# Moving 28 transposes from TensorE to transfers, holding back the first output group, and spreading the rounding of a weight, in a two-layer kernel

## The chip, the cores and the metric

The kernel runs on all 8 cores of one Trainium2 chip. Each core computes one of the 8 sequences of the batch, so the cores do the same work on different data and exchange nothing. The metric is the device time of the slowest core in microseconds (us).

## The reference

The reference is a "sandwich": a gated recurrence, then a feed-forward block with ternary weights and 8-bit activations, each behind a layer norm and added to its input.

```
def attn(x, W_in, W_sel_in, W_sel_out, W_out, d):          # per sequence, 4096 x 1024
    u = x @ W_in.T                                          # 256 states
    gates = silu(x @ W_sel_in.T) @ W_sel_out.T              # 4 x 256
    a, b, c, dg = sigmoid, tanh, tanh, sigmoid of the 4 parts
    h_t = a_t * h_{t-1} + (b*u)_t                           # scan over 4096 tokens
    return (c*h + d*dg*u) @ W_out.T

def ffn(x, w1, conv_w, conv_b, w2):
    h = bit_linear(x, w1)                                   # 4096 hidden channels
    h = silu(depthwise_conv1d(h, width 3, padding 1) + b)
    return bit_linear(h, w2)
# bit_linear: activations rounded to 8 bits with the scale of their own token
# (127/max|x|), weights rounded to -1, 0, 1 by their mean magnitude

x = x + layernorm(attn(layernorm(x)))
x = x + layernorm(ffn(layernorm(x)))
```

## The kernel before

All engines run from lists written in one program order; semaphores order them. **Layer one** takes the first 322 us: `half_step(H)` for 128-token groups. In its gaps a generator, `weight_work()`, loads `w1` and `w2` in pieces of 128 x 1024 fp32 (512 KB), sums their magnitudes, and rounds them to fp8 (`rounded`, L533 and L540: a scale-and-add into `kw`, then a Sign on ScalarE). A call of `next(work, None)` takes one step. When layer one ends, 26 pieces of `w2` are still to be rounded.

**Layer two** works in 8 chunks of 512 tokens, each cut into 32 blocks of 128 hidden channels: 256 *slots* n, one a channel block. A slot does, in program order: 8 matmuls of the first product (`w1_mm`, L721), the evacuation to `hp` (ScalarE, L727), the middle tap (ScalarE, L746), the outer taps and sums (VectorE, L753, L760, L765), SiLU for two slots together (L772), running maximum and minimum (VectorE, L780). 38 slots later, since a token's scale needs all its channels, VectorE multiplies and rounds a 128-token piece m = n - 38 (`quant_mul` L833, `quant_rnd` L839, one slot ahead of its use) and TensorE does 8 matmuls of the second product (`w2_mm`, L850). Eight pieces make an output group Gx of 128 tokens, finished by `fin_stats` (VectorE), `fin_chain` (GpSimd), `fin_apply` (ScalarE, then an fp32 addition on GpSimd, L911) and a store. So slots 0 to 37 hold only the first product on TensorE, slots 38 to 255 hold both, and from slot 256 on only the second runs. The convolution shifts the tokens by one: group 0 holds 127 tokens, and the very last token is left over; `last_hidden` and `last_mm` (L953, 64 matmuls whose stationary operand has one column) do it at the end as a group of its own.

**The next chunk's input** is made in between: a group of 128 tokens is centred (GpSimd, L406), reduced (VectorE L411, ScalarE L415), scaled (ScalarE L435), rounded into `xqmB` (VectorE, `quant_x`, L440), transposed by 8 TensorE instructions into PSUM (`quant_T`, L447) and evacuated to `xqT` (ScalarE, `quant_Tev`, L452). In layer two these steps take slots 0 to 6 of every 8 slots (`gq, r = 4 + n // 8, n % 8`), so 4 groups a chunk, 28 in all; chunk 7 has none to make. At a chunk's start 4 small TensorE transposes and 4 small matmuls (L797, L817) make the token scales of the chunk that ended.

The rounding of `w2` takes one step a slot: GpSimd does L533 and ScalarE L540 in slots 0 to 26. Its staging buffers `stgC` and `kw` lie in the memory that the ring `h4` reuses later; the wait at n == 31 guards that. The residual rows `x2r` have two buffers. SyncE (SP) issues all the transfers of layer two in program order, and a wait of one holds back those behind it.

Of the kernel before, what the change touches and what calls it, by code (L numbers as in the profile page):

```python
# [29 lines left out]
class Q:  # L30
# [38 lines left out]
    def dma(self, en, out, in_, sem, *toks):  # L69
        self.wait(en, *toks, (sem, self.cnt.get(sem, 0)))  # L70
        self.cnt[sem] = self.cnt.get(sem, 0) + 16
        self.q[en].append(lambda e, S: e.dma_start(out=out, in_=in_).then_inc(S[sem], 16))  # L72
        return (sem, self.cnt[sem])
# [5 lines left out]
def build_program():  # L79
# [90 lines left out]
    hxq = sb("hxq", 32, BF16)  # L170
    yev = [sb("yev%d" % k, D, F32) for k in range(2)]
    x2r = [sb("x2r%d" % k, D, F32) for k in range(2)]
# [5 lines left out]
    with st_:  # L178
# [8 lines left out]
        hs4 = hs.ap().rearrange("p (f c t) -> p f c t", f=2, c=32)  # L187
        h43 = h4.ap().rearrange("p (c t) -> p c t", c=NH4)
# [266 lines left out]


# [238 lines left out]
        v_q, p_w2 = Z(NW), Z(NW)  # L695
# [160 lines left out]
        def rows(Gx):  # L856

            if Gx == 0:
                return 1, 128, 0
            if Gx == NG:  # L860
                return 0, 1, T_TOK - 1
            return 0, 128, 128 * Gx - 1

        def load_x2(Gx):
            if Gx > NG:
                return
            p0, p1, r0 = rows(Gx)
            x2_ld[Gx] = q.dma("sy", x2r[Gx % 2][p0:p1, 0:D], x2_h[r0:r0 + p1 - p0, :],
                              "x2l%d" % (Gx % 2), g_fo[Gx - 2] if Gx >= 2 else fin_ready[0],
                              v_x2z[0])  # L870

        def fin_stats(Gx):
            np_ = 1 if Gx == NG else 128
            pb = pairW2[Gx % 2]
            for j in range(12):
                sc("bnF", j)
            c0 = col[("bnF", 0)]
            sc("mF", 0), sc("mF", 1)
            c1 = col[("mF", 0)]
            V(lambda e: e.bn_stats(sm[0:np_, c0:c0 + 6], pb[0:np_, 0:512]),  # L880
              v_fs[Gx - 1] if Gx else None, p_w2[8 * Gx + 7] if Gx < NG else p_last[0])
            t = V(lambda e: e.bn_stats(sm[0:np_, c0 + 6:c0 + 12], pb[0:np_, 512:1024]))
            v_fs[Gx] = V(lambda e: e.bn_aggr(sm[0:np_, c1:c1 + 2], sm[0:np_, c0:c0 + 12]), t,  # L883
                         g_fc[Gx - 1] if Gx else None)

        def fin_chain(Gx):
            np_ = 1 if Gx == NG else 128
            f, g, k = Gx // 4, Gx % 4, Gx % 2
            if Gx == NG:
                g2 = sc("g2x")[0:1, :]  # L890
            else:
# [7 lines left out]
            t = G(lambda e: e.tensor_tensor(rs, eF, nhalf[0:np_, :], OP.pow), t)  # L899
            t = G(lambda e: e.tensor_scalar(rF, rs, g2, None, OP.mult), t)  # L900
            g_fc[Gx] = G(lambda e: e.tensor_scalar(bF, mF, rF, none1[0:np_, :], OP.mult, OP.mult), t)  # L901

        def fin_apply(Gx):
            np_ = 1 if Gx == NG else 128
            k = Gx % 2
            pb, Y, X2 = pairW2[Gx % 2], yev[Gx % 2], x2r[Gx % 2]
            a_fa[Gx] = A(lambda e: e.activation(  # L907
                Y[0:np_, :], pb[0:np_, :], AF.Identity, bias=sc("bF", k)[0:np_, :],
                scale=sc("rF", k)[0:np_, :]),
                d_out[Gx - 2] if Gx >= 2 else fin_ready[0], g_fc[Gx])  # L910
            g_fo[Gx] = G(lambda e: e.tensor_tensor(Y[0:np_, :], Y[0:np_, :], X2[0:np_, 0:D], OP.add),  # L911
# [241 lines left out]
```

## Time and profile before

| | us |
|---|---|
| median of 3 runs (lowest, highest) | 1316.98 (1315.31, 1319.25) |
| the profiled execution, its own time | 1316.7 |
| its span, first to last instruction, slowest core (5) | 1315.2 |
| the eight cores' spans | 1308.8 to 1315.2 |
| TensorE, VectorE, ScalarE, GpSimd busy | 89%, 84%, 65%, 32% |

Shares over the whole span hide that the stages differ: layer one is spent on all engines, slots 0 to 37 on VectorE and ScalarE, and slots 38 to 255 on TensorE. The stretches below are cut at the evacuations (L727) that open a slot, so that each holds whole slots.

### The profile page before, as it was taken

The numbers are of one execution on the slowest core, as the hardware profiler recorded it, in microseconds if no ns is written. First come the engines' busy times: TensorE is split into PE (matmuls) and PEld (weight loads), VectorE is DVE, ScalarE is ACT, GpSimd is POOL, SyncE is SP. The second block draws the span as 40 slices with busy tenths as digits, with TensorE's granted clock in tenths as the row PEclk, the third lists the DMA queues.
The fourth block names the chain that finished last, engine by engine and source line by source line (L and its number), as shares of the span: only waits on it lengthen the run. The fifth ranks groups of instructions, "written<-read, shape, count | busy, mean of one in ns | idle before, by whom it ended". The sixth has DMA issues, their size and how long they took to land.

```text
span 1315.2 us, 18619 instructions; the slowest of 8 cores (1308.8 to 1315.2 us)
## 1 busy us (share of the span) xinstructions
PE 1168.4 (89%) x6184; PEld 603.1 (46%) x6184; DVE 1106.9 (84%) x2302; ACT 855.1 (65%) x1131; POOL 419.2 (32%) x654
## 2 busy tenths in 40 slices
PE   0378898997666899999999999999999999999897
PEld 0256666774222444444444444444444444444442
DVE  0269889986999999999999999999999999888661
ACT  0798989998899666666666666666666666555001
POOL 1114222321774122244333224333322431212233
PEclk9998878888898899999999999999999999999898
DMA  9996689995661112111211111121211111010110
GB/s 206 319 331 218 186 256 292 311 310 185 207 198 44 46 39 75 49 48 50 80 49 65 49 49 49 54 76 48 65 49 49 49 51 47 33 33 33 63 67 33
DMA packets 40099, 146.51 MB, mean 111 GB/s; under 512 B 4804, under 2 KB 4804, under 8 KB 39748
## 3 DMA queue, kind: packets, MB, share of 16 engines
q1 hardware_dynamic: 39572, 142.69, 33.8%
q0 software_dynamic: 432, 2.62, 1.2%
q8 instruction: 51, 0.84, 0.2%
q14 instruction: 44, 0.36, 0.1%
HBM read 114.36 MB, written 33.55 MB: 112 GB/s over the span
## 4 chain that ended last, share of the span: by engine, by line
PE 69%; DVE 16%; ACT 5%; DMA 4%; SPq 2%; issue 2%; POOL 1%; POOLq 0%; DVEq 0%; ACTq 0%
PE pF L850 32%; PE pO L721 27%; DMA stg<-w1T 4%; PE pF L326 4%; SPq L72 2%; DVE h L760 2%; PE pO L372 2%; DVE xs L393 1%; DVE h L765 1%; DVE hsc L356 1%; PE pF L953 1%; DVE h L753 1%; PE pT L447 1%; DVE accP L780 1%; DVE ysb L361 1%
## 5 line engine op out<-in xcount | busy, mean ns | idle before, releaser
L850 PE MATMUL pF<-w2q,h 128*128 128x512 fp8e4 x2048 | 480.1, 380 | 1.8 <-DVE h L839 1.8
L721 PE MATMUL pO<-xqT,w1q 128*128 128x512 bf16 x1792 | 427.1, 382 | 5.6 <-ACT xqT L452 5.6
L850 PEld LDWEIGHTS pF<-w2q,h 128*128 128x128 bf16 x2048 | 200.6, 98 | 241.8 <-issue 4.6
L727 ACT ACTIVATE hp<-pO 128x512 bf16<-128x512 f32 x224 | 133.6, 596 | 218.8 <-PE pO L721 217.4
L721 PEld LDWEIGHTS pO<-xqT,w1q 128*128 128x128 fp8e4 x1792 | 175.2, 98 | 213.8 <-issue 10.8
L760 DVE SCALAR_TENSOR_TENSOR h<-hp,cwt,h 128x512 bf16<-128x512 bf16 x256 | 202.8, 792 | 0.7
L746 ACT ACTIVATE bt<-hp,cwt 128x512 bf16<-128x512 bf16 x256 | 183.9, 718 | 6.1
L772 ACT ACTIVATE h<-h 128x1024 bf16<-128x1024 bf16 x128 | 134.9, 1054 | 76.1 <-DVE h L765 75.7
L833 DVE TENSOR_TENSOR h<-h,bc 128x512 bf16<-128x512 bf16 x256 | 151.0, 590 | 0.0
L896 POOL TENSOR_SCALAR sm<-sm 128x1 f32<-128x1 f32 (+1 forms) x33 | 17.2, 522 | 376.6 <-DVE sm L883 376.6
L765 DVE TENSOR_TENSOR h<-h,bt 128x512 bf16<-128x512 bf16 x256 | 115.6, 452 | 14.7 <-ACT bt L746 1.3
L753 DVE TENSOR_SCALAR h<-hp,cwt,cbt 128x512 bf16<-128x512 bf16 x256 | 111.9, 437 | 15.2 <-ACT hp L727 14.7
L911 POOL TENSOR_TENSOR yev<-yev,x2r 128x1024 f32<-128x1024 f32 (+1 forms) x33 | 78.1, 2368 | 45.4 <-ACT yev L907 45.4
L721 PE MATMUL pF<-xqT,w1q 128*128 128x512 bf16 x256 | 66.6, 412 | 29.2 <-ACT hp L727 25.4
L780 DVE TENSOR_TENSOR accN<-accN,h 128x1024 bf16<-128x1024 bf16 x120 | 92.0, 767 | 0.0
L907 ACT ACTIVATE yev<-pF,sm 128x1024 f32<-128x1024 f32 (+1 forms) x33 | 39.6, 1200 | 78.6 <-POOL sm L901 78.6
L780 DVE TENSOR_TENSOR accP<-accP,h 128x1024 bf16<-128x1024 bf16 x120 | 82.1, 684 | 0.1
L741 POOL COPY hs<-hp 128x8 bf16<-128x8 bf16 x64 | 25.8, 403 | 167.4 <-ACT hp L727 167.4
L326 PE MATMUL pF<-selh,wsoT_b 128*128 128x256 bf16 x512 | 70.7, 306 | 4.4 <-ACT selh L319 4.4
L839 DVE TENSOR_SCALAR h<-h 128x512 bf16<-128x512 bf16 x256 | 73.4, 287 | 1.2
L285 PE MATMUL pT<-identb,xn 128*128 128x128 bf16 x256 | 24.6, 253 | 54.1 <-ACT xn L278 52.8
L308 PE MATMUL pF<-xinT,wselT_b 128*128 128x256 bf16 x512 | 65.9, 294 | 0.0
(147 smaller groups left out, 1514.7 us busy)
## 6 DMA issues: line engine op xcount, KB each, us to landing
stg<-w1T SPq DMA_DIRECT2D x40, 512.0 KB, 15.3
xs<-x SPq DMA_DIRECT2D x32, 512.0 KB, 11.2
stg<-w2T SPq DMA_DIRECT2D x32, 512.0 KB, 9.1
x2c<-xs SPq DMA_DIRECT2D x32, 512.0 KB, 9.0
stgC<-w2T SPq DMA_DIRECT2D x32, 512.0 KB, 5.9
x2r<-x2c SPq DMA_DIRECT2D x31, 512.0 KB, 4.6
out<-yev SPq DMA_DIRECT2D x31, 512.0 KB, 3.0
x2q<-x2c SPq DMA_DIRECT2D x28, 512.0 KB, 3.3
```

The lines of the kernel that those rows point to most:

```text
L326: t = P(lambda e, gi_=gi_, m=m, k=k: e.matmul(pF[:, at + 256 * gi_:at + 256 * (gi_ + 1)], wsoT[:, 1024 * k + 128 * m:1024 * k + 128 * (m + ...
L721: p_w1[n] = P(lambda e, k=k: e.matmul(bankW1(n), w1q[:, HD * k + 128 * c:HD * k + 128 * (c + 1)], xT[:, :, k, :], start=(k == 0), stop=(k ...
L727: a_ev[n] = A(lambda e: e.activation(hp3[:, n % 8, 2:514], bankW1(n), AF.Identity), *((v_stt[n - 8], a_bt[n - 8], g_sv[n // 4 - 2]) if n > ...
L746: a_bt[n] = A(lambda e: e.activation(bt[n % 3][:, :], hp3[:, n % 8, 1:513], AF.Identity, scale=cwt[:, 3 * c + 1:3 * c + 2]), v_cv[n - 3] i ...
L753: v_ts[n] = V(lambda e: e.tensor_scalar(H_, hp3[:, n % 8, 0:512], cwt[:, 3 * c:3 * c + 1], cbt[:, c:c + 1], OP.mult, OP.add), p_w2[32 * (o ...
L760: v_stt[n] = V(lambda e: e.scalar_tensor_tensor(H_, hp3[:, n % 8, 2:514], cwt[:, 3 * c + 2:3 * c + 3], H_, OP.mult, OP.add), v_ts[n])
L765: v_cv[n] = V(lambda e: e.tensor_tensor(H_, H_, bt[n % 3][:, :], OP.add), v_stt[n], a_bt[n])
L772: a_si[n] = a_si[n - 1] = A(lambda e: e.activation(pair(n), pair(n), AF.Silu), v_cv[n])
L780: t = V(lambda e: e.tensor_tensor(acc[:, :], acc[:, :], pair(n), o), mm_tok[which], a_si[n])
L833: q_tok[m] = V(lambda e: e.tensor_tensor(piece(m), piece(m), bc2[f % 2][:, 128 * g:128 * (g + 1)].unsqueeze(1).to_broadcast([128, 4, 128]) ...
L850: p_w2[m] = P(lambda e, c=c, jj=jj: e.matmul(pb[:, 512 * jj:512 * (jj + 1)], h43[:, ring(32 * f + c), 128 * g:128 * (g + 1)], w2q[:, D * c ...
L911: g_fo[Gx] = G(lambda e: e.tensor_tensor(Y[0:np_, :], Y[0:np_, :], X2[0:np_, 0:D], OP.add), x2_ld[Gx], a_fa[Gx])
```

## The change

- **Transposes by transfer.** In layer two `quant_T` and `quant_Tev` (8 TensorE instructions, one ScalarE instruction) become `turn_x`: one transposing transfer on SP from `xqmB` to `xqT`. The next `quant_x` and the next chunk's first product wait for its semaphore. The first 4 groups, in layer one, stay on TensorE.
- **Cadence.** The steps of a group now start every 7 slots within the first 28 slots of a chunk (`gq, r = 4 + 4 * f1 + s1 // 7, s1 % 7`).
- **First group held back.** Group 0's rounded values go to a buffer of their own, `held` (m < 8), and its 64 matmuls are not done in slots 38 to 45 but at the very end; the last token takes the place of its unused first column. So `last_mm` and one of 33 finishing groups are gone.
- **Rounding of w2.** The same steps are spread over 42 slots, and the waits move to n == 47. Its buffers and four of `xs` change places in memory.
- **The end.** The last group's application and addition are cut in halves, the addition is on VectorE, and six smaller stores follow (`fin_end`). `x2r` has one buffer and its clearing at n == 31 is gone. In layer one, mean and variance go to small columns instead of behind `xs`.

```diff
@@ transposes
-            if r == 5:
-                quant_T(gq, xqmB, pT1b, pT1_free)
-            if r == 6:
-                quant_Tev(gq, xqT[gq // 4 % 2][:, D * (gq % 4):D * (gq % 4 + 1)], pT1b, pT1_free,
+            if r == 5:
+                turn_x(gq, xqT[gq // 4 % 2][:, D * (gq % 4):D * (gq % 4 + 1)], xqmB,
+        def turn_x(gi, dst, xqm, *toks):
+            p_t2[gi] = a_t2[gi] = q.dma("sy", dst.rearrange("p (k t) -> p k t", k=8), xqm[:, :],
+                                        "tx", v_xq[gi], *toks, turn=True)
-            gq, r = 4 + n // 8, n % 8
-            if gq < NG:
+            gq, r = 4 + 4 * f1 + s1 // 7, s1 % 7
+            if gq < NG and s1 < 28:
@@ the first group
+            dst = held3[:, 4 * m:4 * m + 4, :] if m < 8 else piece(m)
-            if 0 <= m < NW:
+            if 8 <= m < NW + 8:
                 w2_mm(m)
-            if m == NW:
-                last_mm()
@@ w2's rounding
+        left = len(steps) + 1 - at_step[0]
-            next(work, None)
+            if n < 42 and (n + 1) * left // 42 > n * left // 42:
+                next(work, None)
+            if n == 47:
+                q.wait("v", v_w2q[31], *kw_free)
-                v_x2z[0] = V(lambda e: e.memset(x2r[0][0:1, :], 0.0))
@@ the end
-        fin_apply(NG)
-        fin_store(NG)
+        fin_end()
+            for n in range(2):
+                h = slice(512 * n, 512 * (n + 1))
+                t = V(lambda e, h=h: e.tensor_tensor(Y[:, h], Y[:, h], X2[:, h], OP.add),
+                      *x2_ld[Gx], toks[n])
+                for i, (p0, p1, r0) in enumerate(rows(Gx)):
+                    q.dma("sy", out_h[r0:r0 + p1 - p0, h], Y[p0:p1, h], "oe%d" % (3 * n + i), t)
```

TensorE in chunk 1, slots 51 to 54, before: `pO` is the first product, `pF` the second, `pT` the transposes.

```order
L850 MATMUL pF<-w2q,h_111 128x512 x8
L721 MATMUL pO<-xqT_112,w1q 128x512 x8
L850 MATMUL pF<-w2q,h_111 128x512 x8
L447 MATMUL pT<-identb,xqmB 128x128 x8
L721 MATMUL pO<-xqT_112,w1q 128x512 x8
L850 MATMUL pF<-w2q,h_111 128x512 x8
```

And now, the same engine and stage:

```order
L734 MATMUL pO<-xqT_112,w1q 128x512 x8
L868 MATMUL pF<-w2q,h_111 128x512 x8
L734 MATMUL pO<-xqT_112,w1q 128x512 x8
L868 MATMUL pF<-w2q,h_111 128x512 x8
L734 MATMUL pO<-xqT_112,w1q 128x512 x8
```

The eight transposes are gone from between the products.

GpSimd in slots 4 to 12 of chunk 0, before: `kw` is the first half of w2's rounding, `x2q` the centring of a group, `hp` and `hs` the carried columns.

```order
L735 COPY hp<-hs 128x4x2
L533 TENSOR_SCALAR kw_63<-stgC_66,wcons,consts 128x1024
L533 TENSOR_SCALAR kw_64<-stgC_65,wcons,consts 128x1024
L533 TENSOR_SCALAR kw_63<-stgC_68,wcons,consts 128x1024
L533 TENSOR_SCALAR kw_64<-stgC_67,wcons,consts 128x1024
L741 COPY hs<-hp 128x8
L735 COPY hp<-hs 128x4x2
L406 TENSOR_SCALAR x2q_124<-x2q_124,nmean,ones 128x1024
```

And now:

```order
L748 COPY hp<-hs 128x4x2
L543 TENSOR_SCALAR kw_67<-stgC_72,wcons,consts 128x1024
L543 TENSOR_SCALAR kw_68<-stgC_71,wcons,consts 128x1024
L411 TENSOR_SCALAR x2q_124<-x2q_124,nmean,ones 128x1024
L543 TENSOR_SCALAR kw_67<-stgC_70,wcons,consts 128x1024
L754 COPY hs<-hp 128x8
L748 COPY hp<-hs 128x4x2
```

Between two restores (4 slots) stand 2 or 3 roundings instead of 4; the 26 roundings reach into slot 41.

SP around two groups of chunk 2, now (before, only the load of `x2q`, the store and the load of `x2r` stood there):

```order
L73 DMA x2q_124<-x2c 128x1024 [waits dv,xq1]
L73 DMA_TRANSPOSE xqT_112<-xqmB 128x8x128 [waits tx]
L73 DMA out<-yev_129 128x1024 [waits gp,ot0]
L73 DMA x2r<-x2c 128x1024 [waits x2l0]
L73 DMA x2q_123<-x2c 128x1024 [waits dv,xq0]
L73 DMA_TRANSPOSE xqT_112<-xqmB 128x8x128 [waits tx]
```

The transposing transfer stands in the one queue of SP, between loads and stores.

## Rows read from the trace of the kernel before

**Rows 1.** The page: the chain that ended last, shares by engine.
```profile
PE 69%; DVE 16%; ACT 5%; DMA 4%; SPq 2%; issue 2%; POOL 1%; POOLq 0%; DVEq 0%; ACTq 0%
```

**Rows 2.** Windows: stretch, its length, busy of each engine (instructions), clock, DMA.
```profile
351.10:376.05 24.95, 17.23 (x74) 6.49 (x72) 24.36 (x39) 24.15 (x34) 20.10 (x16) 0.93 0.61 190
376.05:400.95 24.90, 17.22 (x74) 6.64 (x72) 24.31 (x39) 24.15 (x33) 20.04 (x16) 0.93 0.55 169
400.95:423.00 22.05, 12.26 (x52) 4.62 (x50) 20.55 (x39) 19.44 (x29) 7.74 (x10) 0.88 0.07 25
423.00:442.87 19.87, 15.36 (x69) 7.50 (x68) 16.17 (x38) 11.41 (x17) 4.64 (x5) 0.79 0.22 73
442.87:470.94 28.07, 28.07 (x137) 12.95 (x138) 27.21 (x64) 18.48 (x27) 4.03 (x7) 1.00 0.07 25
```

**Rows 3.** Windows, the same columns: chunk 2, eight slots with, eight without transposes.
```profile
564.38:678.80 114.42, 113.81 (x557) 52.90 (x556) 107.20 (x237) 72.94 (x101) 38.00 (x53) 1.00 0.17 56
592.45:620.53 28.08, 28.08 (x137) 12.99 (x136) 25.77 (x56) 18.29 (x26) 10.22 (x14) 1.00 0.17 58
1135.00:1162.63 27.63, 27.63 (x129) 12.54 (x128) 24.92 (x55) 15.43 (x22) 6.97 (x12) 1.00 0.12 39
```

**Rows 4.** Timeline, TensorE: start, length; the first transposes behind slot 46 and the last.
```profile
496.83 0.61 PE L447 MATMUL pT<-identb,xqmB 128*128 128x128 bf16 x8
...
1096.98 0.61 PE L447 MATMUL pT<-identb,xqmB 128*128 128x128 bf16 x8
```

**Rows 5.** Timeline, GpSimd and VectorE in slots 14 to 16, and slot 31.
```profile
369.59 4.30 POOL L533 TENSOR_SCALAR kw<-stgC,wcons,consts 128x1024 f32<-128x1024 f32 x2 [1.88 <-ACT w2q L540]
...
370.02 0.75 DVE L760 SCALAR_TENSOR_TENSOR h<-hp,cwt,h 128x512 bf16<-128x512 bf16 x1
371.62 1.22 DVE L753 TENSOR_SCALAR h<-hp,cwt,cbt 128x512 bf16<-128x512 bf16 x1
372.87 1.56 DVE L760 SCALAR_TENSOR_TENSOR h<-hp,cwt,h 128x512 bf16<-128x512 bf16 x1
374.88 0.41 DVE L753 TENSOR_SCALAR h<-hp,cwt,cbt 128x512 bf16<-128x512 bf16 x1
...
421.57 0.91 DVE L1058 MEMSET x2r<- 1x1024 f32 x1 [0.19 <-issue]
```

**Rows 6.** The waits: engine, tile, line, releaser: us, times, longest; second product.
```profile
PE pF L850 <- DVE h L839: 1.8, 2, 1.3
```

**Rows 7.** DMA issues: count, KB each, median us to landing.
```profile
x2q<-x2c SPq DMA_DIRECT2D x28, 512.0 KB, 3.3
x2r<-x2c SPq DMA_DIRECT2D x31, 512.0 KB, 4.6
stgQ<-w1T SPq DMA_DIRECT2D x7, 512.0 KB, 21.2
```

**Rows 8.** Timeline, the last microseconds, and a half-width fp32 operation of VectorE.
```profile
300.92 0.69 DVE L359 TENSOR_TENSOR ch<-bcg,hsc 128x512 f32<-128x512 bf16 x1
...
1291.99 13.97 PE L953 MATMUL pF<-w2q,hxq 128*1 128x512 fp8e4 x64
...
1309.81 1.20 ACT L907 ACTIVATE yev<-pF,sm 1x1024 f32<-1x1024 f32 x1 [12.63 <-POOL sm L901]
1311.09 2.33 POOL L911 TENSOR_TENSOR yev<-yev,x2r 1x1024 f32<-1x1024 f32 x1 [1.31 <-ACT yev L907]
```

**Rows 9.** Timeline, TensorE: a first product at either clock, after a wait and in steady state.
```profile
433.35 3.62 PE L721 MATMUL pO<-xqT,w1q 128*128 128x512 bf16 x8
...
609.52 1.89 PE L850 MATMUL pF<-w2q,h 128*128 128x512 fp8e4 x8
```

More of the change, by code:

```diff
@@ L67, in op, with dma @@
         return (sem, self.cnt[sem]) if inc else None
-    def dma(self, en, out, in_, sem, *toks):
+    def dma(self, en, out, in_, sem, *toks, turn=False):
         self.wait(en, *toks, (sem, self.cnt.get(sem, 0)))
         self.cnt[sem] = self.cnt.get(sem, 0) + 16
-        self.q[en].append(lambda e, S: e.dma_start(out=out, in_=in_).then_inc(S[sem], 16))
+        kind = {"transpose": True} if turn else {}
+        self.q[en].append(lambda e, S: e.dma_start(out=out, in_=in_, **kind).then_inc(S[sem], 16))
         return (sem, self.cnt[sem])
@@ L131, in build_program @@
     place[0] = both_end + 32 * 1024
+    xs = [sb("xs%d" % k, D, F32) for k in range(4)]
     kw = [sb("kw%d" % k, D, F32) for k in range(2)]
@@ L169, in build_program @@
     hx = sb("hx", 64, F32)
-    hxq = sb("hxq", 32, BF16)
+    held = sb("held", 32 * 128, BF16)
     yev = [sb("yev%d" % k, D, F32) for k in range(2)]
-    x2r = [sb("x2r%d" % k, D, F32) for k in range(2)]
+    x2r = sb("x2r", D, F32)
     b_end = place[0]
@@ L262, in ln1_stats @@
             X, k = slot(gi), gi % 2
-            both = cols("bn1", k, 12)
+            both, mv = cols("bn1", k, 12), cols("m1", k, 2)
             old = v_st1[gi - 2] if gi >= 2 else None
@@ L845, in w2_mm @@
             pb = pairW2[Gx % 2]
-            q.wait("t", v_q[m], *(v_w2q[4 * j:4 * j + 4] if m < 8 else ()),
-                   a_fa[Gx - 2] if Gx >= 2 and j == 0 else None)
+            q.wait("t", v_q[m] if Gx < NG else v_hxq[0],
+                   *(v_w2q[4 * j:4 * j + 4] if Gx == 1 else ()),
+                   a_fa[Gx - 2] if Gx >= 3 and j == 0 else None)
             for c in range(4 * j, 4 * j + 4):
+                hid = (held3[:, c, :] if Gx == NG else
+                       h43[:, ring(32 * f + c), 128 * g:128 * (g + 1)])
                 for jj in range(2):
-                    p_w2[m] = P(lambda e, c=c, jj=jj: e.matmul(
-                        pb[:, 512 * jj:512 * (jj + 1)],
-                        h43[:, ring(32 * f + c), 128 * g:128 * (g + 1)],
+                    p_w2[m] = P(lambda e, c=c, jj=jj, hid=hid: e.matmul(
+                        pb[:, 512 * jj:512 * (jj + 1)], hid,
                         w2q[:, D * c + 512 * jj:D * c + 512 * (jj + 1)],
@@ L903, in fin_apply @@
         def fin_apply(Gx):
-            np_ = 1 if Gx == NG else 128
             k = Gx % 2
-            pb, Y, X2 = pairW2[Gx % 2], yev[Gx % 2], x2r[Gx % 2]
+            pb, Y, X2 = pairW2[Gx % 2], yev[Gx % 2], x2r
             a_fa[Gx] = A(lambda e: e.activation(
[L908 to L911, printed above, removed]
-                         x2_ld[Gx], a_fa[Gx])
@@ L945, in last_hidden @@
             t2 = V(lambda e: e.tensor_scalar(X0, X0, mc, RC, OP.mult, OP.add), t2)
[L946 to L958 removed]
+            v_hxq[0] = V(lambda e: e.tensor_scalar(held3[:, :, 0], X0, -RC, None, OP.add), t2, v_q[7])
+        fin_ready = [None]
         load_x2q(4)
```

116 lines of the change are left out of this document (56 added, 60 removed).

## The prediction

> **What bounds the kernel now.** I read the chain of waits first, then the busy time by stretch, then single rows. The chain [rows 1] says TensorE for 69% of the span, but that is an average; the stretches say where. In chunk 0 (slots 8 to 23) VectorE and ScalarE are both busy for 24.1 to 24.4 of 24.9 us per 8 slots, and TensorE for 17.2 [rows 2]. So there eight slots cost what VectorE and ScalarE need, 3.1 us a slot. From slot 38 on the picture turns round: TensorE is busy for all of the 28.07 us of 8 slots, and VectorE for 27.21 in slots 38 to 45 [rows 2] and 107.20 of 114.42 us in a later chunk [rows 3]. The second product waits for VectorE for 1.8 us in the whole span [rows 6]. TensorE is the bound in slots 38 to 255, with VectorE at 94% close behind. The tail (only second products) is TensorE's too.
>
> I make the sum against the profiled execution (1316.7 us, span 1315.2), which is 0.3 us from the median of the runs, 1316.98; a saving in it is taken off the median.
>
> **Transposes.** Eight slots of a chunk with a group to make take 28.08 us, eight slots of the last chunk, which has none, 27.63 [rows 3]: 0.45 us for 8 transposes, though each set shows 0.61 of its own [rows 4], since matmuls overlap their neighbours' ends. From slot 46 to the end of chunk 6 there are 22 such sets, the first and last of them in [rows 4]. TensorE bounds there, so 22 x 0.45 = 9.9 us go, if nothing else is late. What is late next is VectorE: a chunk would take 114.42 - 4 x 0.45 = 112.6 us of TensorE, against 107.2 of VectorE, 95%. The steps of four groups now stand in 28 slots instead of 32, and in slot 22 a reduction falls into the slot in which an output group's statistics are taken. For such bunches I put +1 us over six chunks, with 0 and +5 as the ends. ScalarE loses its evacuations; it has a third of its time free in chunk 2 (72.94 of 114.42), so this gives nothing.
>
> **The transfer that replaces them** is in no row. It moves 256 KB. The nearest rows by size and load are loads of 512 KB that land in 3.3 and 4.6 us at a DMA share of 0.17; the slowest of SP's transfers, under a full load in layer one, take 21.2 us [rows 7]. So I bound it by 1.6 and 21 us and take 5. Its cover: `xqmB` is rewritten 7 slots later, 7 x 3.45 = 24 us, and the last group of a chunk is issued in slot 26 and first read in slot 32, about 20 us. In chunk 0, at 2.9 us a slot, the same distance is 17 us, and TensorE runs a few slots ahead there, which takes it to about 10. At 5 us all of it is hidden; at 21 us only the chunk ends show, 7 x 1 us or so, plus some 10 us once in chunk 0. On SP it waits for `quant_x`, for which the load before it already waits; what stands behind it are the store and the load of `x2r`. The single buffer of `x2r` is loaded in 4.6 us, and its next use is 8 slots (27 us), in the tail 13.8 us, after the last: hidden.
>
> The rows price eight transposes at 0.45 us of TensorE, and the transfer at less than its cover. The Trainium skill speaks against the swap: "VectorE: DVE Perf Modes", section "The three transpose paths", gives 390 ns for a 128 x 128 transpose on TensorE and 1309 ns by transfer, and its rules advise TensorE where PSUM will do. By that eight would be, as an estimate, 10.5 us of transfer; that is still under the cover of 20 to 24 us in the steady chunks, and the sum would stay. No row here shows the transfer.
>
> **The first group.** 64 matmuls leave slots 38 to 45, 13.8 us of TensorE, and 64 return at the end in place of the 64 of the last token (13.97 us [rows 8]). The tail is so unchanged in TensorE. In slots 38 to 45 TensorE would need half of the 28.07 us, but VectorE keeps its 27.21 [rows 2], because the rounding of group 0 is still done there. So of 13.8 us only the 0.86 us by which VectorE was idle can be won: this edit has nearly no worth of its own, and I count it with the next.
>
> **The head, slots 0 to 45.** A rounding of `w2` costs VectorE time too, though it runs on GpSimd and ScalarE: beside an L533 on GpSimd, L753 goes from 0.41 to 1.22 us and L760 from 0.75 to 1.56 [rows 5]. From 350.3 to 375.2 eight operations of VectorE are longer by 5.9 us together, beside 8 roundings and a centring: 0.65 us each. Spreading 26 roundings over 42 slots does not remove this, it moves it: 9 or 10 of them go to slots 27 to 41, 6.3 us of VectorE later for 6.3 us earlier. What can be won is time in which VectorE was idle: 0.59, 0.59, 1.50, 3.70 and 0.86 us in the five stretches of [rows 2], 7.2 us, and the clearing of `x2r` (0.9 us [rows 5]). In the first two stretches ScalarE was as full as VectorE; it now gets 1.05 us x 0.36 less a slot and drops out as a bound. Of the 3.70 us about half are waits across the chunk's end that stay. I take 4.0 us as gained. The ends are -8 us (all of it) and +5 us: if slots 0 to 26 do not get shorter by what leaves them, because something else holds them, the 6.3 us added behind slot 26 remain, less the clearing.
>
> **The clock.** TensorE is half busy until slot 45 instead of slot 37. In 423 to 443 us, busy 15.4 of 19.9, it was granted 0.79, and one set of 8 matmuls took 3.62 us instead of 1.89 [rows 2, 9]; these are the 1.2 and the 2.4 GHz level. If slot 46 opens at the lower one, a set or two cost 1.7 us each: 0 to +3.5, I take +0.5.
>
> **The end.** After the last matmul the chain is as before up to L907 at 1309.81. Then 1.20 + 2.33 us of application and addition [rows 8] become two halves of about 0.6 and two additions of 0.69 (L359), about 2.1 us to the last, against 3.6; three issues more at about 0.35 us and larger stores take back most of the difference. -0.3 (-1 to +0.5).
>
> **Sum.** -9.9 + 1.0 - 4.0 + 0.5 - 0.3 = -12.7 us. 1316.98 - 12.7 = 1304.3.
>
> **The rivals.**
> *VectorE takes over in the steady chunks.* It is at 94%; if bunching or GpSimd work at a new phase adds 5.5 us to its 107.2, the chunk ends at VectorE's time and the transposes give nothing: -12.7 + 8.9 = -3.8, 1313.2. For it: every longer GpSimd operation stretches a VectorE one by 0.8 us [rows 5]. Against: nothing in the change adds VectorE work, and the second product waits for it for 1.8 us in all [rows 6].
> *The head gets longer.* Roundings in slots 27 to 41 are on VectorE's path, and slots 0 to 26 are held by another thing, such as the chain GpSimd, ScalarE, GpSimd of the rounding (waits of 1.88 us before an L533 [rows 5]). Then +5 instead of -4: -3.7, 1313.3. Against: that chain has fewer links per slot now.
> *It gets slower: the transfer outlasts its cover.* Each group waits for the one before through `xqmB`. Over 24 us, every us costs 24 groups 1 us each: at 30 us +139 us in the steady chunks, so some 1450. It turns the gain into a loss from about 24.6 us on. Against: no row of 512 KB took that long, even at a DMA share near 1; for it: no row shows a transposing transfer, and moving elements of 2 bytes could be far slower than rows of 4 KB.
> *The held group pays.* Without second products VectorE and TensorE might pass slots 38 to 45 faster than 27 us, if VectorE's operations there were stretched by waiting rather than by work: up to 7 us more, 1297.3. Against: 27.21 of 28.07 us are busy.
>
> **How the numbers follow.** Forecast 0.66, VectorE takes over 0.12, head longer 0.10, transfer outlasts 0.07, held group pays 0.05. The gaining ends of all terms together are -9.9 - 8 - 1 = -18.9 us, 1298.1, and one more of the losing ends (VectorE's +5 or the head's +5) beside the taken values gives 1313.3 at most; I leave out the transfer's case and two losing ends at once: 1298 to 1313.5. A difference of 0.3% (4 us) is about what a measurement of this kernel tells from none. Faster by more than that: the forecast, the last rival, half of the first two: 0.82; within: 0.11; slower: 0.07.
>
> **What would show it.** In the profile after: eight slots of chunks 1 to 6 at 27.63 us, TensorE busy without gaps, no transposes between them; VectorE at 95 to 97% of a chunk. Slots 8 to 23 at 2.8 to 2.9 us instead of 3.1, with ScalarE at 80 to 90%. Slots 38 to 45 at about 27 us with TensorE half busy. The second product's first matmul about 4 us before 470.9. The transposing transfers landing in under 10 us, and no wait of `quant_x` or the first product for them. Wrong would be: waits of the second product for VectorE of more than 5 us in all, or any wait for `xqT`.

## The result: 0.4% slower, and where it went

The changed kernel takes 1322.56 us (median of 6 runs, 1321.61 to 1323.05) against 1317.14 us of the kernel before beside it: the ratio is 1.0042, 95% interval 1.0031 to 1.0053. Forecast were 1304.3 us and a range that ended at 1313.5. Repeated later on another chip the ratio was 1.0047 (1.0034 to 1.0060). Executions in which the cores of one die ran at a lower granted clock and took some per cent longer are left out of every ratio.

The page of the changed kernel, its first line and the chain that ended last (by engine, then by line):

```profile
span 1321.3 us, 18079 instructions; the slowest of 8 cores (1312.9 to 1321.3 us)
...
DVE 38%; PE 34%; ACT 8%; DMA 7%; issue 6%; POOL 3%; SPq 2%; DVEq 0%; POOLq 0%; ACTq 0%
PE pF L868 17%; PE pO L734 12%; DVE h L773 7%; DVE h L778 5%; DVE h L766 4%; DMA stg<-w1T 4%; DVE accP L793 3%; ACT h L785 3%; DMA x2c<-xs 2%; SPq L73 2%; DVE h L846 2%; DVE xqmB L445 2%; DVE sm L416 2%; PE pF L331 2%; ACT hp L740 2%
```

This is the first thing to see. Before, TensorE had 69% of the chain and VectorE 16% [rows 1]; now VectorE leads with 38%. The chain is no sum of causes, but followed back through 560 to 680 us, which lies in chunks 2 and 3, it says the same of the steady chunks: the two products had 91% of it there and have 23% now. VectorE has taken a large part of TensorE's place.

The windows of the same kernel, cut at the evacuations that open a slot (stretch, length, busy time of TensorE, its weight loads, VectorE, ScalarE, GpSimd with instructions, clock, DMA share, GB/s): slots 8 to 15, 16 to 23, 24 to 31 of chunk 0, then chunk 2 from slot 8 on over 32 slots, and two stretches of 8 slots in it.

```profile
352.51:377.38 24.87, 18.28 (x70) 6.66 (x67) 24.28 (x40) 21.49 (x32) 13.11 (x15) 0.90 0.43 137
377.38:400.44 23.06, 14.45 (x63) 5.75 (x64) 22.09 (x41) 20.37 (x29) 16.05 (x13) 1.00 0.42 127
400.44:422.19 21.75, 13.01 (x51) 4.87 (x48) 21.19 (x34) 19.56 (x27) 13.58 (x10) 0.92 0.55 167
561.75:677.93 116.18, 112.84 (x525) 50.70 (x524) 107.96 (x236) 69.74 (x96) 36.14 (x53) 1.00 0.24 64
590.63:618.44 27.81, 27.81 (x129) 12.39 (x128) 26.79 (x58) 17.06 (x24) 8.88 (x13) 1.00 0.23 67
618.44:648.13 29.69, 27.95 (x129) 12.40 (x128) 27.92 (x63) 16.60 (x23) 9.62 (x16) 1.00 0.22 63
```

Against [rows 3]: 32 slots took 114.42 us and take 116.18, though TensorE's work in them is less. Slots 16 to 23 still run at 27.81, near the 27.63 of the forecast; the next eight need 29.69, with VectorE busy for 27.92 of them and TensorE standing for 1.7.

Cut at slots 48, 224 and 248, the two profiled executions compare like this:

| stretch | before, us | changed, us | difference | forecast |
|---|---|---|---|---|
| layer one, start to slot 0 | 322.34 | 323.37 | +1.0 | 0 |
| head, slots 0 to 47 | 155.70 | 153.25 | -2.5 | -3.5 |
| slots 48 to 223 | 628.22 | 635.72 | +7.5 | -8.9 |
| slots 224 to 247 | 83.99 | 84.00 | 0.0 | 0 |
| slot 248 to the end of the span | 124.91 | 124.97 | +0.1 | -0.3 |

These two executions differ by 6.1 us where 12.7 less was forecast, a miss of 18.8 us, and 16.4 of it stands in slots 48 to 223. The first row is hardly an effect of the change: on one other chip four kernels, two with each version of layer one, reached slot 0 between 317.6 and 319.9 us, at 318.2 in the mean with the new version and at 319.3 with the old.

Inside a chunk the loss has a place. Four slots take 13.8 us when TensorE alone sets the pace (the table's values are differences between starts of evacuations, L727 or L740, in chunk 2; every chunk from 2 to 6 shows the same within 0.4 us):

| slots of the chunk | 0-3 | 4-7 | 8-11 | 12-15 | 16-19 | 20-23 | 24-27 | 28-31 | chunk |
|---|---|---|---|---|---|---|---|---|---|
| before | 14.8 | 15.4 | 13.8 | 14.3 | 13.8 | 14.3 | 13.8 | 14.3 | 114.41 |
| changed | 14.8 | 15.0 | 15.1 | 13.8 | 14.0 | 13.8 | 15.9 | 13.8 | 116.14 |

The transposes' 0.45 us are gone from every eight slots, and two bulges have come, 1.3 us in slots 8 to 11 and 2.1 us in slots 24 to 27. The timeline of the changed kernel in slots 22 to 26 of chunk 2 (start, length, engine, line, what, and the wait before it):

```profile
619.72 0.22 DVE L433 TENSOR_SCALAR sm<-sm 128x1 f32<-128x1 f32 x1 [1.70 <-POOL sm L428]
...
621.76 0.75 DVE L773 SCALAR_TENSOR_TENSOR h<-hp,cwt,h 128x512 bf16<-128x512 bf16 x1
...
622.84 2.81 POOL L912 TENSOR_TENSOR yev<-yev,x2r 128x1024 f32<-128x1024 f32 x1 [2.88 <-ACT yev L909]
...
623.36 2.84 DVE L445 TENSOR_SCALAR xqmB<-x2q,sm 128x1024 bf16<-128x1024 f32 x1
...
627.21 1.89 PE L868 MATMUL pF<-w2q,h 128*128 128x512 fp8e4 x8 [1.60 <-DVE h L853]
```

VectorE waits 1.70 us for the scale of an input group (L428), since GpSimd was doing the chain of an output group (from 616.1 to 618.8); then the long fp32 addition on GpSimd (L912) overlaps the rounding of the input group (L445), which takes 2.84 us instead of 0.75; the piece for the second product is 1.6 us late. In the whole span:

```profile
PE pF L868 <- DVE h L853: 15.9, 12, 1.9
PE pO L734 <- ACT hp L740: 13.2, 6, 4.9
```

The first line was 1.8 us, 2 times before [rows 6]. The visible waits of TensorE understate the loss.

### The profile page after: what moved, and what is told of

It is laid out like the page before. It is cut to its first block, busy times and chain, and to the rows that moved or that the text cites. A ratio compares the mean times of both kernels' runs of the same rounds, so it can differ in the third digit from the quotient of the medians.

```text
span 1321.3 us, 18079 instructions; the slowest of 8 cores (1312.9 to 1321.3 us)
## 1 busy us (share of the span) xinstructions
PE 1136.8 (86%) x5896; PEld 576.1 (44%) x5896; DVE 1109.1 (84%) x2301; ACT 831.0 (63%) x1103; POOL 405.8 (31%) x647
## 4 chain that ended last, share of the span: by engine, by line
DVE 38%; PE 34%; ACT 8%; DMA 7%; issue 6%; POOL 3%; SPq 2%; DVEq 0%; POOLq 0%; ACTq 0%
PE pF L868 17%; PE pO L734 12%; DVE h L773 7%; DVE h L778 5%; DVE h L766 4%; DMA stg<-w1T 4%; DVE accP L793 3%; ACT h L785 3%; DMA x2c<-xs 2%; SPq L73 2%; DVE h L846 2%; DVE xqmB L445 2%; DVE sm L416 2%; PE pF L331 2%; ACT hp L740 2%
## 5 line engine op out<-in xcount | busy, mean ns | idle before, releaser
L868 PE MATMUL pF<-w2q,h 128*128 128x512 fp8e4 x1984 | 464.6, 380 | 16.5 <-DVE h L853 15.9
L868 PEld LDWEIGHTS pF<-w2q,h 128*128 128x128 bf16 x1984 | 191.9, 98 | 255.0 <-issue 32.4
L740 ACT ACTIVATE hp<-pO 128x512 bf16<-128x512 f32 x224 | 132.5, 591 | 142.2 <-PE pO L734 141.2
L773 DVE SCALAR_TENSOR_TENSOR h<-hp,cwt,h 128x512 bf16<-128x512 bf16 x256 | 213.8, 835 | 0.7
L766 DVE TENSOR_SCALAR h<-hp,cwt,cbt 128x512 bf16<-128x512 bf16 x256 | 118.7, 464 | 9.2 <-ACT hp L740 9.2
L846 DVE TENSOR_TENSOR h<-h,bc 128x512 bf16<-128x512 bf16 x256 | 122.6, 479 | 0.0
L899 POOL TENSOR_SCALAR sm<-sm 128x1 f32<-128x1 f32 x32 | 15.7, 490 | 334.1 <-DVE sm L891 334.1
L912 POOL TENSOR_TENSOR yev<-yev,x2r 128x1024 f32<-128x1024 f32 x31 | 79.1, 2553 | 50.0 <-ACT yev L909 49.8
L793 DVE TENSOR_TENSOR accN<-accN,h 128x1024 bf16<-128x1024 bf16 x120 | 90.7, 756 | 0.0
L793 DVE TENSOR_TENSOR accP<-accP,h 128x1024 bf16<-128x1024 bf16 x120 | 83.8, 699 | 0.1
L909 ACT ACTIVATE yev<-pF,sm 128x1024 f32<-128x1024 f32 x31 | 37.2, 1199 | 65.3 <-POOL sm L904 65.3
L377 PE MATMUL pO<-woutT_b,ysb 128*128 128x512 bf16 x128 | 35.3, 400 | 44.4 <-DVE xs L398 43.6
L853 DVE TENSOR_SCALAR h<-h 128x512 bf16<-128x512 bf16 x248 | 71.4, 288 | 1.2
L290 PE MATMUL pT<-identb,xn 128*128 128x128 bf16 x256 | 23.8, 247 | 51.8 <-ACT xn L283 51.0
```

The costliest lines, as they stand in the source:

```text
L740: a_ev[n] = A(lambda e: e.activation(hp3[:, n % 8, 2:514], bankW1(n), AF.Identity), *((v_stt[n - 8], a_bt[n - 8], g_sv[n // 4 - 2]) if n > ...
L766: v_ts[n] = V(lambda e: e.tensor_scalar(H_, hp3[:, n % 8, 0:512], cwt[:, 3 * c:3 * c + 1], cbt[:, c:c + 1], OP.mult, OP.add), p_w2[32 * (o ...
L773: v_stt[n] = V(lambda e: e.scalar_tensor_tensor(H_, hp3[:, n % 8, 2:514], cwt[:, 3 * c + 2:3 * c + 3], H_, OP.mult, OP.add), v_ts[n])
L793: t = V(lambda e: e.tensor_tensor(acc[:, :], acc[:, :], pair(n), o), mm_tok[which], a_si[n])
L846: q_tok[m] = V(lambda e: e.tensor_tensor(piece(m), piece(m), bc2[f % 2][:, 128 * g:128 * (g + 1)].unsqueeze(1).to_broadcast([128, 4, 128]) ...
L868: p_w2[m] = P(lambda e, c=c, jj=jj, hid=hid: e.matmul(pb[:, 512 * jj:512 * (jj + 1)], hid, w2q[:, D * c + 512 * jj:D * c + 512 * (jj + 1)] ...
```

## The experiments

All ratios are against runs of the kernel before on the same chip. Three theories stood against each other: (A) the new cadence of 7 slots lets a group's steps meet an output group's steps; (B) the transposing transfers disturb the other engines; (C) VectorE has no room below 114 us a chunk whatever the order.

**Cadence 8 in the changed kernel** (`e1_cadence8`).

```diff
-            gq, r = 4 + 4 * f1 + s1 // 7, s1 % 7
-            if gq < NG and s1 < 28:
+            gq, r = 4 + n // 8, n % 8
+            if gq < NG:
```

> The changed kernel with the cadence of before (a group's steps in slots 0 to 6 of every 8), everything else as changed. In the changed kernel four slots of a chunk take 13.8 us where nothing stands in the way, but slots 8 to 11 take 15.1 and slots 24 to 27 take 15.9; before no four slots behind slot 8 took over 14.3. Theory A, the cadence: steps of a group meet the statistics and the long addition of an output group in the same slots, and VectorE falls behind. Then both bulges go, a chunk takes 112.7 us instead of 116.1, and the time is 1322.5 - 3.5 x 5.5 = about 1303. Theory B, the transposing transfers disturb VectorE or ScalarE: the chunk stays near 116 and the time near 1322. Theory C, VectorE has no room below 114 us a chunk whatever the cadence: 114.4 us a chunk, about 1312.

Measured: ratio 0.990 (0.988 to 0.992), the profile's span 1298.7 us. Slots 48 to 223 took 618.40 us, 17.3 less than in the changed kernel. The windows of this kernel, chunk 2:

```profile
526.56:639.19 112.63, 112.02 (x525) 51.06 (x524) 104.14 (x236) 69.80 (x96) 38.70 (x53) 1.00 0.22 66
```

The chunk takes 112.63 us, which is the 112.6 of the forecast, and TensorE is busy for all but 0.6 of it. Both bulges are gone with the transfers still there. B and C fall. For a kernel of 1317 us the ratio is 1304, where about 1303 was expected.

**Cadence 7 in the kernel before** (`e2_before_cadence7`), the same two lines the other way round, transposes on TensorE.

> The kernel before with the cadence of 7 slots only; transposes stay on TensorE. Theory A: the same bulges at slots 8 to 11 and 24 to 27, a little smaller as TensorE is slower by 0.45 us a group: a chunk takes 117 to 118 us instead of 114.4, the time is about 1332. Theory B: no bulge, the time stays at 1317. Theory C: VectorE's work is the same, 1317.

Measured: 1.0082 (1.0065 to 1.0099). A chunk took 116.5 us, with 15.6 in slots 24 to 27 and 14.6 in slots 8 to 11. The cadence alone, without any transfer, makes both bulges. They are smaller than expected (1332 was expected, 1.0082 is 1328 for a kernel of 1317); that TensorE's own 0.45 us a group leaves VectorE more room would explain it, but is not shown.

**The transfers alone in the kernel before** (`e3_before_turn`): `turn_x` at r == 5 in place of `quant_T` and `quant_Tev`.

```diff
-                    quant_T(gq, xqmB, pT1b, pT1_free)
-                if r == 6:
-                    quant_Tev(gq, xqT[gq // 4 % 2][:, D * (gq % 4):D * (gq % 4 + 1)], pT1b, pT1_free,
+                    turn_x(gq, xqT[gq // 4 % 2][:, D * (gq % 4):D * (gq % 4 + 1)], xqmB,
```

> The kernel before with the transposing transfers only, cadence 8. Theory A: 0.45 us of TensorE a group go, a chunk takes 112.7 us, the time is 1317 - 10 = 1307. Theory B: bulges where the transfers run, 1322 or more. Theory C: 1317.

Measured: 0.9930 (0.9914 to 0.9947), about 9 us. Slots 48 to 223 went from 628.22 to 618.45 us, 9.8, against 9.9 forecast for the transposes; all 22 sets that the forecast counted lie in these slots. What a transfer costs, by the DMA issues of the changed kernel (count, median us to landing) and the transfers' own lines in the changed kernel with cadence 8 (its issues on SP in ns, its landings min, median, max):

```profile
xqT<-xqmB SPq DMA_TRANSPOSE x28, 4.3
```

```profile
L73 SPq DMA_TRANSPOSE xqT<-xqmB x28: 1237/1237/1751, 336.5 to 1075.1; - x28
...
DMA to landing us min/median/max: 3.1/4.3/6.4
```

**The second and the last start moved, one at a time.** First the last group of a chunk starts in slot 24, the others stay at 0, 7 and 14 (`e5_last_at24`):

```diff
-            gq, r = 4 + 4 * f1 + s1 // 7, s1 % 7
-            if gq < NG and s1 < 28:
+            gq, r = NG, 0
+            for i_, at_ in enumerate((0,7,14,24)):
+                if at_ <= s1 < at_ + 7:
+                    gq, r = 4 + 4 * f1 + i_, s1 - at_
+            if gq < NG:
```

> The changed kernel with its groups starting in slots 0, 7, 14 and 24 of a chunk instead of 0, 7, 14 and 21. If each bulge belongs to one group's start (21 makes slots 24 to 27, 7 makes slots 8 to 11): the bulge at 24 to 27 goes from 15.9 to 13.8 us, the one at 8 to 11 stays at 15.1; a chunk takes 114.0 us and the time is 2.1 x 5.5 = 12 us below the changed kernel, 0.995 of the kernel before. If instead it is the sum of VectorE's work in the chunk, both change.

Measured: 0.9970 (0.9957 to 0.9982), beside the changed kernel's 1.0047 on that chip. In chunk 2, slots 24 to 27 took 13.8 us, slots 8 to 11 stayed at 15.1, the chunk took 114.05. The trace is as forecast. The time fell by 9.8 us (1321.74 to 1311.96, medians), and slots 48 to 223 by 10.2, where I had said 12: 2.1 us in the five chunks 2 to 6 are 10.5, and chunk 1 had no bulge of that size (13.8 us in its slots 24 to 27 in the repeated run of the changed kernel).

Then the second group starts in slot 8, the others stay at 0, 14 and 21 (`e10_second_at8`):

```diff
+            for i_, lo_, hi_ in ((0, 0, 7), (1, 8, 14), (2, 14, 21), (3, 21, 28)):
+                if lo_ <= s1 < hi_:
+                    gq, r = 4 + 4 * f1 + i_, s1 - lo_
```

> The changed kernel with the second group of a chunk starting in slot 8 instead of 7; the others stay at 0, 14 and 21. By the bulge of each start: slots 8 to 11 fall from 15.1 to 13.8 us, slots 24 to 27 stay at 15.9; a chunk takes 114.8 us and the time is 7 us under the changed kernel, 0.999 of the kernel before.

Measured: 0.9982 (0.9972 to 0.9992). Slots 8 to 11: 13.8 us, slots 24 to 27: 15.5, the chunk 114.37, where 114.8 was expected. The bulges are apart and each belongs to one start, but for 0.4 us of the later one, which went with the move of the second group too.

**What in the cadence does it.** The long addition of the output groups on GpSimd is cut to 8 of its 1024 columns (groups 1 to 31; the output lacks the rest), once with cadence 7 (`e7_no_addition`), once with cadence 8 (`e11_cadence8_no_addition`):

```diff
-            g_fo[Gx] = G(lambda e: e.tensor_tensor(Y[:, :], Y[:, :], X2[:, 0:D], OP.add),
+            g_fo[Gx] = G(lambda e: e.tensor_tensor(Y[:, 0:8], Y[:, 0:8], X2[:, 0:8], OP.add),
```

> The changed kernel (cadence 7) without the long fp32 addition of the residual rows on GpSimd in the output groups 1 to 31: it covers 8 of 1024 columns, so the output lacks the rest. In slot 24 that addition (2.8 us) overlaps the rounding of an input group on VectorE, which takes 2.84 us instead of 0.75. If this overlap makes the bulges: the one at slots 24 to 27 falls from 15.9 to 14.3 us or less and the one at 8 to 11 from 15.1 to under 14; a chunk takes 113 us, the time is 1305. If VectorE's own work in a bunch makes them (statistics and reduction in one slot, 2.5 us), the bulges stay above 15 us and the time above 1316.

> The control to the run without the addition: cadence 8 throughout, and the addition of the residual rows covers 8 of 1024 columns in the output groups 1 to 31, so the output lacks the rest. With cadence 7 and without the addition a chunk took 111.76 us. If the cadence costs only through the addition, this is the same: a chunk 111.7 to 111.8 us, 0.987 of the kernel before. If the cadence costs something by itself, it is shorter than that.

Measured: 0.9872 (0.9852 to 0.9892) with cadence 7, 0.9842 (0.9824 to 0.9861) with cadence 8. A chunk took 111.77 and 111.62 us: without the addition the cadence costs 0.15 us a chunk, with it 3.5. Slots 24 to 27 took 13.8 us and slots 8 to 11 took 14.0 with cadence 7. The effect is larger than expected (113 us a chunk and 1305), since slots 0 to 3 of a chunk became 0.8 us shorter as well. The lines of a chunk by source (count, busy us, mean ns, idle before) say why. The changed kernel, chunk 2:

```profile
L773 DVE SCALAR_TENSOR_TENSOR h<-hp,cwt,h 128x512 bf16<-128x512 bf16 x32 | 26.7, 835 | 0.0
L846 DVE TENSOR_TENSOR h<-h,bc 128x512 bf16<-128x512 bf16 x32 | 15.0, 468 | 0.0
L912 POOL TENSOR_TENSOR yev<-yev,x2r 128x1024 f32<-128x1024 f32 x4 | 10.3, 2563 | 5.8 <-ACT yev L909 5.7
L445 DVE TENSOR_SCALAR xqmB<-x2q,sm 128x1024 bf16<-128x1024 f32 x4 | 5.1, 1273 | 0.1
```

With cadence 8, chunk 2:

```profile
L773 DVE SCALAR_TENSOR_TENSOR h<-hp,cwt,h 128x512 bf16<-128x512 bf16 x32 | 23.8, 745 | 0.0
L846 DVE TENSOR_TENSOR h<-h,bc 128x512 bf16<-128x512 bf16 x32 | 18.8, 586 | 0.0
L912 POOL TENSOR_TENSOR yev<-yev,x2r 128x1024 f32<-128x1024 f32 x4 | 9.4, 2354 | 1.4 <-ACT yev L909 1.4
L445 DVE TENSOR_SCALAR xqmB<-x2q,sm 128x1024 bf16<-128x1024 f32 x4 | 3.0, 751 | 0.7 <-ACT x2q L440 0.6
```

With cadence 7 and no addition:

```profile
L773 DVE SCALAR_TENSOR_TENSOR h<-hp,cwt,h 128x512 bf16<-128x512 bf16 x32 | 24.6, 769 | 0.0
L445 DVE TENSOR_SCALAR xqmB<-x2q,sm 128x1024 bf16<-128x1024 f32 x4 | 3.0, 748 | 0.5 <-ACT x2q L440 0.5
L912 POOL TENSOR_TENSOR yev<-yev,x2r 128x8 f32<-128x8 f32 x4 | 1.5, 377 | 8.1 <-ACT yev L909 8.1
```

The means hide what each addition does, and the timeline shows it. With cadence 8, from slot 8 of chunk 2 on (start, length, engine, line):

```profile
559.06 2.35 POOL L912 TENSOR_TENSOR yev<-yev,x2r 128x1024 f32<-128x1024 f32 x1
559.12 1.22 DVE L416 TENSOR_REDUCE sm<-x2q 128x1 f32<-128x1024 f32 x1 [1.10 <-POOL x2q L411]
560.26 1.43 DVE L846 TENSOR_TENSOR h<-h,bc 128x512 bf16<-128x512 bf16 x1
```

And in the changed kernel, the same slots:

```profile
562.33 1.22 DVE L416 TENSOR_REDUCE sm<-x2q 128x1 f32<-128x1024 f32 x1 [1.95 <-POOL x2q L411]
564.73 2.49 POOL L912 TENSOR_TENSOR yev<-yev,x2r 128x1024 f32<-128x1024 f32 x1 [2.16 <-ACT yev L909]
564.93 2.83 DVE L773 SCALAR_TENSOR_TENSOR h<-hp,cwt,h 128x512 bf16<-128x512 bf16 x1
```

The reduction of an input group (L416) takes its 1.22 us beside an addition as without one. The operation that follows it is stretched (L846 usually takes 0.42 us), but only until the addition is over. With cadence 8, and in the kernel before, a reduction stands beside every addition of chunks 2 to 6, 20 of 20; in the changed kernel beside 5 of 20, and elsewhere the whole addition falls on an operation that it stretches: L773 in slots 8 to 11, L793 in 16 to 19, L445 in 24 to 27, each by 2.1 us. Summed over a chunk, VectorE's operations beside the additions take 5.6 us more than their usual time with cadence 8, 7.0 in the kernel before (where the reduction is often nearly over when the addition starts) and 8.0 in the changed kernel. The moves of the last group to slot 24 and of the second to slot 8 each put one more reduction beside an addition, and bring the sum to 7.0 and 7.1.

The other part is what else stands near. In the fourth group the addition falls behind the reduction, the statistics and the wait for GpSimd; in the second behind a late reduction (the wait of 1.95 us above). In slots 16 to 19 the same 2.1 us of stretch stand alone, and those slots took only 14.0 us instead of 13.8. The one slot by which VectorE runs ahead does not cover the sum. That the addition is needed for the bulges is shown. That the wait is needed too is argued from the timeline, and taking the addition away also frees GpSimd for 2.35 us, so the stretch was not tested apart from GpSimd's being late.

**The rounding of w2, one step a slot again,** in the changed kernel (`e4_after_w2_slot`) and with cadence 8 (`e6_cadence8_w2_slot`):

```diff
-            if n < 42 and (n + 1) * left // 42 > n * left // 42:
-                next(work, None)
-            if n == 47:
-                assert next(work, None) is None
-                q.wait("v", v_w2q[31], *kw_free)
+            next(work, None)
             if n == 31:
-                q.wait("v", *d_x2[NG - 5:NG])
+                q.wait("v", v_w2q[31], *kw_free, *d_x2[NG - 5:NG])
```

> The changed kernel with the rounding of w2 as before, one step a slot from slot 0 on. It prices the spreading. If the spreading gave what the head gained (slot 48 is reached 2.4 us earlier after the start of layer two than before), this is 2 to 4 us slower than the changed kernel, 1325. If the spreading only moved the roundings' cost on VectorE, it is the same, 1322.5.

> The changed kernel with cadence 8 and with the rounding of w2 one step a slot, as before. If spreading the rounding gains in the head, 1 to 2 us slower than with cadence 8 alone (which was 0.990 of the kernel before). If it costs, as the changed kernel with the old rounding (1.0022 against 1.0042) hints, about 2 us faster, 0.988 to 0.989. In the trace the head (slot 0 to 48) says it: 152.5 us with cadence 8 and the spreading.

Measured: 1.0022 (1.0012 to 1.0033) where the changed kernel had 1.0042 (1.0031 to 1.0053), and 0.9909 (0.9894 to 0.9924) where cadence 8 alone had 0.990 (0.988 to 0.992). On the slowest cores the heads (slot 0 to 48) were 154.0 and 152.1 us, against 153.3 and 154.8 in two runs of the changed kernel and 152.5 with cadence 8. The head differs from core to core by up to 3.4 us within one execution, so the medians of the eight cores say more: without the spreading 151.4 with either cadence, with it 153.7 and 154.7 (cadence 7, the two runs) and 152.1 (cadence 8). The spreading gains nothing; by these medians it costs 0.8 us with cadence 8 and 2 to 3 with cadence 7, and both ratios of cadence 7 agree with that.

**The 64 matmuls of the held group put back** into slots 38 to 45, in addition to those at the end (`e8_cadence8_mm_back`); their results are not used:

```diff
+            if 0 <= m < 8:
+                q.wait("t", v_q[m], *v_w2q[4 * m:4 * m + 4])
+                for c_ in range(4 * m, 4 * m + 4):
+                    for jj_ in range(2):
+                        P(lambda e, c=c_, jj=jj_: e.matmul(
+                            pairW2[0][:, 512 * jj:512 * (jj + 1)], held3[:, c, :],
```

> The changed kernel with cadence 8, and in slots 38 to 45 the 64 matmuls of the held group are done as well, in addition (their result there is not used; they are 13.8 us of TensorE). My theory, that VectorE bounds these slots: the head gets 0.5 to 1.5 us longer, time 0.991. Rival, TensorE's time counts: up to 13.8 us longer, 1.000.

Measured: 0.9925 (0.9912 to 0.9939), and the head 155.4 us instead of 152.5: 2.9 us. Slots 40 to 47 of the kernel with cadence 8, then of this one:

```profile
446.75:471.31 24.56, 17.74 (x80) 7.27 (x79) 23.99 (x57) 17.88 (x26) 7.37 (x10) 1.00 0.13 33
```

```profile
449.92:477.54 27.62, 27.62 (x129) 12.54 (x128) 27.05 (x60) 18.12 (x25) 6.64 (x9) 1.00 0.12 29
```

With the matmuls TensorE is full, 27.62 of 27.62 us; without them the same slots take 24.56. So the held group pays 2.9 of its 13.8 us, more than the 0.5 to 1.5 that I expected and far less than the rival said. VectorE is busy nearly throughout in both, with 60 and 57 instructions between the two evacuations. That is no slower VectorE: from the rounding of piece 3 to that of piece 11 (L853) it took 23.89 us with the matmuls and 23.80 without. With them it worked ahead of TensorE; without them TensorE ran up to it and waited 1.7 us for the rounding of piece 8.

**Cadence 7 in chunk 0, cadence 8 behind it** (`e9_mixed`):

```diff
+            gq, r = (4 + n // 7, n % 7) if n < 28 else (4 + n // 8, n % 8)
+            if gq < NG and not 28 <= n < 32:
```

> The changed kernel with cadence 7 in chunk 0 alone and cadence 8 in chunks 1 to 6. With cadence 8 throughout, the first product waits once for the transposing transfer at the end of chunk 0, about 5 us of TensorE; with the earlier last group of cadence 7 it does not. If this wait is on the path, 1 to 3 us faster than cadence 8 alone (0.990 of the kernel before), 0.988; if VectorE holds the head anyway, the same 0.990.

Measured: 0.9898 (0.9883 to 0.9912), the same as cadence 8 throughout; head 153.6 us. The earlier last group of chunk 0 buys nothing. That VectorE holds the head is the likely reason; it was not tested apart.

**The changed kernel beside these runs** (`e0_after_again`).

> The changed kernel itself, beside the others on one chip. Both theories of the cadence: 0.4% over the kernel before, as at first. Its head (slot 0 to slot 48) about 153 us, a chunk 116.1.

Measured: 1.0047 (1.0034 to 1.0060); chunk 2 took 116.15 us, the head 154.8.

## Why the prediction was wrong, step by step

**What bounds the kernel: right.** TensorE in slots 38 to 255, VectorE at 94% behind it. The second half of that sentence decided the case.

**The transposes: right.** 22 sets at 0.45 us were 9.9 us; the run with the transfers alone gave 9.8 in slots 48 to 223 and a ratio of 0.993.

**The transfer: right.** Assumed 5 us between 1.6 and 21; it landed in 4.3 us in the changed kernel (3.1 to 7.9), with 1.22 us of SP's time. In the other kernels the medians were 4.2 to 4.7 us; the slowest two landed in 10.7 and 16.6 us, both in the kernel before with the transfers alone, where SP was held by them for 4.7 and 10.8 us. No wait for `xqT` stands in the changed kernel; in five of the others TensorE waited for it once, for 4.8 to 7.0 us in the head, and the kernel with cadence 7 in chunk 0 alone, which has no such wait, had no shorter head. The Trainium skill ("VectorE: DVE Perf Modes", section "The three transpose paths") led to an estimate of 10.5 us for eight blocks; here eight blocks in one transfer land in less than half of that, 0.54 us a block. The Trainium skill's advice to take TensorE where PSUM will do (same title, section "Rules for kernel authors") does not hold for this kernel, where TensorE is the bound and the transfer has 20 us of cover.

**The bunching: the step that failed.** The forecast named the place: "in slot 22 a reduction falls into the slot in which an output group's statistics are taken", and put +1 us on it over six chunks, with +5 as the end. It measured 3.5 us a chunk, 17.3 us in slots 48 to 223, between the changed kernel and the same with cadence 8. The prediction's own sign of being wrong, waits of the second product for VectorE of more than 5 us in all, came at 15.9. Two things were wrong in the sizing. I compared sums over a chunk (VectorE 107.2 of 112.6 us) where the buffer between the engines is one slot, so that the sum over three or four slots counts. Slots 22 to 25 could have been added up roughly from the rows of the kernel before: four slots' own work at about 2.55 us (an estimate from starts of VectorE's operations in slots without extras, 2.05 and 3.05 us in turn), a reduction of 1.2, statistics of 1.5, the small operations and the rounding of a group 1.2, and an addition's stretch of 2 us, some 16.1 us in 13.8 of TensorE. And I treated GpSimd's stretch of VectorE as fixed work that moves without harm. It is not fixed: 7.0 us a chunk before, 8.0 with cadence 7, 5.6 with cadence 8, by how much of each addition a reduction covers. And where the rival put 0.8 us on each longer GpSimd operation, an addition costs 1.0 to 2.1. I had used a stretch of this kind to price the head.

**The rival "VectorE takes over": right in mechanism, too small.** It was given 0.12 and 1313.2 us, on the reasoning that the transposes could at worst give nothing. The chunk's time is not the larger of two sums: bulges add to TensorE's time, as it does not catch up afterwards. So the floor of the rival, steady chunks as long as before, was wrong by 7.5 us (slots 48 to 223), and the range ended there.

**The head: near in sum, wrong in cause.** Forecast -4.0 to slot 46, measured -2.5 to slot 48. I gave most of it to the spreading of the rounding, which gains nothing and rather costs, and at most 0.86 us to the held group, which is worth 2.9. The place says the same: slots 0 to 37 took 121.8 us before and 122.9 after, slots 38 to 47 took 34.0 and 30.4. Slots 16 to 23 did fall to 2.9 us a slot, as forecast, but slots 8 to 15 stayed at 3.1. VectorE's 27.21 busy of 28.07 us [rows 2] was read as what those slots need of it. That stretch is cut where TensorE begins a second product (442.87 and 470.94), not at evacuations, and in it VectorE also works ahead of TensorE: from the rounding of piece 3 to that of piece 11 it took 25.9 us there, and 23.8 and 23.9 in the two runs that price the held group. So TensorE, and not VectorE, held these slots before. Cadence 7 together with the spreading also costs the head something: medians of the eight cores of 153.7 to 154.8 us in five runs with both, 151.4 to 152.2 in four with only one of them or neither. Why the two together cost more was not looked into.

**The clock.** Slot 46 opened at the full clock in both kernels (1.00, the 2.4 GHz level), so the 0.5 us taken for a slow start of it was not there. Between 443 and 470 us the granted clock was 0.87, against 1.00 before; what this cost was not taken apart.

**The end: not told from nothing.** From slot 248 on the medians of the eight cores are 124.3 to 124.7 us in the three kernels with the old end and 123.9 to 125.2 in the nine with the new one and the whole addition, so the -0.3 is neither borne out nor refuted.

The best kernels of this study with a full output are the changed one with cadence 8, 1.0% faster than the kernel before (0.988 to 0.992), and its two near relatives (0.9898 and 0.9909), which the intervals do not tell from it.

## What to carry to other kernels

Where two engines are both above 90%, compare their work over the length of the buffer between them, here one slot, and not over the period: the second engine's bunches add to the first one's time. A cadence of steps has a phase against every other cadence in the loop; 8 against 8 keeps it, 7 against 8 moves it by a slot with every group, and the worst phase is paid in every chunk. The phase also decides which operation meets a long one on GpSimd: put one there that does not slow down. An edit that frees the bound engine should be made and timed apart from an edit that moves work on the engine next behind it.

## What the runs showed of the hardware

One transposing transfer of 128 x 1024 bf16 within SBUF landed in 4.3 us in the changed kernel (3.1 to 7.9) and held SP for 1.22 us, against 0.32 to 0.38 us for a plain one of 512 KB; over all kernels the slowest took 16.6 us. No stretch was seen on VectorE from it: in the kernel before with the transfers alone a chunk with four of them took 112.64 us, TensorE's own pace, and its second outer tap took 746 ns in the mean, against 745 without them (L760).

An fp32 addition of 128 x 1024 on GpSimd (2.35 us) stretches most VectorE operations that meet it: ones of 0.42, 0.69, 0.75 and 0.75 us became 2.2, 2.8, 2.8 and 2.8, and each ended 0.3 to 0.55 us after the addition. The fp32 reduction of 128 x 1024 was not stretched: it took 1.20 to 1.22 us in all 20 meetings of chunks 2 to 6 with cadence 8, and in all 20 in the kernel before. Without the four additions a chunk of 112.63 us took 111.62.

Busy time near 97% of a stretch did not say how much of the engine the stretch needed: VectorE read 27.05 us in 27.62 with TensorE full and 23.99 in 24.56 with TensorE at 17.74 of them, while its own pace over eight pieces was the same, 23.9 and 23.8 us. A stretch cut at another engine's instructions holds whatever this engine happens to do meanwhile.
